# Fourteen transformer sublayers on one core: identity matmuls with unread results taken out of TensorE's orders

## The chip, the cores and the metric

The kernel runs on one core of one Trainium2 chip, in one launch. The metric is the device time of that core in microseconds (us), lower is better. The engines are named as in the profile: PE is TensorE, DVE is VectorE, ACT is ScalarE, POOL is GpSimd and SP is SyncE. Each has its own instruction queue and runs it in order; they meet over semaphores.

## The reference

The input x is 4 sequences of 512 tokens of width 128. The reference runs twelve sublayers with residuals over it, x + sublayer(layernorm(x)), in a sandwich pattern: a half-weighted feed-forward, an attention, the same feed-forward again, at four levels.

```
x = x + 0.5 * L0_ffn(LN(x)); x = x + L0_attn(LN(x)); x = x + 0.5 * L0_ffn(LN(x))
x = x + 0.5 * L1_ffn(LN(x)); x = x + L1_attn(LN(x)); x = x + 0.5 * L1_ffn(LN(x))
x = x + 0.5 * L2_ffn(LN(x)); x = x + L2_attn(LN(x)); x = x + 0.5 * L2_ffn(LN(x))
x = x + 0.5 * L3_ffn(LN(x)); x = x + L3_attn(LN(x)); x = x + 0.5 * L3_ffn(LN(x))
```

- L0_ffn scores 1024 patterns, takes the top eighth, then the top of 512 processing units, a softmax, and the top of 1024 output patterns. "Top" is found by ranking. L0_attn is causal with relative positions, 16 heads of width 8.
- L1_ffn is itself a causal attention and a mixture of 8 experts with the top 2. L1_attn is a linear causal attention: normalized q and k, a gate beta, no softmax.
- L2_ffn is a mixture of 8 experts with the top 1; L2_attn is causal inside blocks of 32 tokens, with rotation.
- L3_ffn is two transformer layers (8 heads of 64, windows of 64, a gated feed-forward); L3_attn is full attention with rotation.

## The kernel before

**Units and slots.** The twelve sublayers become 14 (each L3_ffn is two layers), and each is done per sequence, except that L2_ffn takes two at a time: 52 units in all. Every unit has three parts. The *pre* part normalizes and makes the heads, the *core* part does the attention or the ranking, the *post* part projects and adds to x. Slot k runs the core of unit k, the pre part of unit k+1 and the post part of unit k-1 side by side. Slots run from -1 to 52. Slots -1 to 2 are blocks of their own, each ended by a barrier; from slot 3 on one block holds all.

**Streams and orders.** In a slot each of those parts is a stream of generator functions, one for each engine. A stream is a letter: a is the core (where there is one), b the pre part, c the post part, and further letters are small extras. A generator's step ends at a `yield`. `in_order` (line 202) runs the steps of an engine in an order written out by hand in the table ORDERS (line 2558): "a5b1" means five steps of stream a, then one of b. SLOT_ORDERS maps the slot to its entry. An engine can't overtake in this order: if the next step waits, all behind it waits.

**The fillers.** The last letter of TensorE's order in twelve of the slots is a stream of its own, made by `fillers` (line 257). Each of its steps is one matmul of the bf16 identity with two copies of the identity, 256 columns:

```
nc.tensor.matmul(out, m.identb, m.identb.unsqueeze(1).to_broadcast([P, FILL // P, P]), start=True, stop=True)
```

The result goes to the right half of a PSUM bank that is not in use in that slot (bank 2, 3, 4, 5 or 6), and is never read. It signals nothing. How many there are is counted from the order string:

```
n = sum(c for i, c in runs(order) if i == len(streams))
```

The first filler of a slot first waits for the end of the core part of the slot before, as the stream is given `before.core`. A filler costs a weight load and a matmul on TensorE and nothing on any other engine.

**Lines that come up.** L265 is the filler matmul. In the L0_ffn: L388 are the four transposes after the normalization (all sublayers use it), L886 the scores of the 1024 patterns (16 matmul instructions, 512 columns), L839 to L842 VectorE's comparisons for the ranking and L850 to L852 the matmuls that sum them, L945 and L1036 the matmuls of its core. In the attentions: L439 makes q, k and v, L586 turns the stacked heads (L550 and L598 copy them out of PSUM), L1456 and L1470 belong to the core of L0_attn, L1747, L1760 and L1765 to that of L1_attn. L663 is the projection of an attention's output. In the last unit's post part: L2502 is the first matmul of the gated feed-forward (six groups of 512 columns, each drained by ScalarE at L2518 or by VectorE at L2530 before the next may start), L2508 the second one (24 matmuls), L307 its bias row.

Of the kernel before, what the change touches and what calls it, by code (L numbers as in the profile page):

```python
# [2461 lines left out]
def l3_layer_post(nc, m, lane, a, b, l):  # L2462
# [82 lines left out]
    def done(eng):  # L2545
        eng.wait_ge(lane.taken, lane.n)
        if l == DEPTH - 1:
# [10 lines left out]
ORDERS = [  # L2558
    {"tensor": "b17a1b3a1b2a1b6a1b1a5b1a2b20a1b3a1b6a1b6a1b1a1b9a1b4a1b2a1",
     "vector": "a13",  # L2560
     "scalar": "a11",
     "gpsimd": "a1"},
# [12 lines left out]
     "scalar": "c2b2a1b7a1b2a1",  # L2575
     "gpsimd": "b1",
     "sync": "f9d1f13e1d1f2a1f8"},
    {"tensor": "a5b1a1b1a1b1a1b1d7b1d12c2d1b1d6c1b2a1d1c1d2a1d4b1c1d4a1d1a1b1d2a1d6b1a1c1a1d3b1d1c1d1a1d6b1a2b1d1b1c"
               "1b1a1b1c2a1c1a1d10",
     "vector": "b4a2b5a1c2a1b1a1c1a1b1a1c2a1b1c2b1c3b1",  # L2580
     "scalar": "b3a1b4c1b1c1b1a1b7a1",
     "gpsimd": "b6",
     "sync": "b1a1b4"},
    {"tensor": "a1b1a1d1b1d1c1d4b1d1b1d1a1d2b1c1d7b1a1c1d1a1b1d7a2b1d1a1d10b1d2c1d1c1d1b1d1a2d1c1a1d1b1d3a1d3b1a1d1a"
               "1c1b1d1a1d4b1a1c1b1d7b1d1c1d1a1d1b1c1d13c1a1d1a2d2a2d3a1d1a1",
     "vector": "b3a1b1a6b5c2a2b1a1c1a3b1c1a3b1c1a2b1c2a2c1a3b1c1a1c1",
     "scalar": "b7a1c1a1c1b2a2b1a2b1a3b1a2b4a9",
     "gpsimd": "b6",
     "sync": "a4b5"},
    {"tensor": "b1c1a1b1e2c1e1b1e5b1e3b1e1a1e2a1e2c1e24b1e9b1e9b1e7a1e3b1e2a3b1a1c1e3b1e2a2b1e2a1e3b1e1c1e3a1e1b1a2b"  # L2590
               "1a1b1c1b1a3e1a2e5a3e5a1",
     "vector": "b4c1b1a1c1b3a1c1b1a4b1a3b1a4b1a1c1a3b1a7c1b1",
     "scalar": "b9a2b1a2b1a2b1a2c1a1b1a2b2a1b1a8",
     "gpsimd": "b6d1",
     "sync": "a4b5"},
    {"tensor": "b1c1b1a2e1b1a1e1b1e2c1b1e35c1a1e4a1e10c1b1e14b1e3b1e3a1e3a1b1a1e1c1e1b1e2c1b1e4a2b1e1a1e5a1b1e1a1e1a"
               "1e1b1e8b1a1e1b1e2a2e1b1e3a1e1a1e7a1e2a3e1a1",
     "vector": "b4c1a5c1a1b4c1b1a2c1a2b1a1b1a4b1a3b1c1a4b1a2",
     "scalar": "b4a1b5a3b1c1b1a4b1a2b1a1b2a2b1a7",
     "gpsimd": "b4d1b2",  # L2600
     "sync": "a4b5"},
    {"tensor": "e5c1b1e2a1b1e1c1e2a1e8b1e7b1c1e2b2e3b1e1a1b1e4a1e4a1e2c1e7b1a2e2a1e3b1e5b1e1a1e2a1e4c1a2e2b1e1b1e4b1"
               "e3a1e9b1e1a1e1b1a3b1e27b1e2a1c1a1e1b1e7a3e1a1e2a1",
     "vector": "b4a1c1a3c2a8c1a3b2a1b1a2b2a1b1a2b1a2b1a1c1b1",
     "scalar": "b7a4b2a1b1a1b1a3c1a11",
     "gpsimd": "d1b1",
# [3 lines left out]
     "scalar": "b11a2c1a1",  # L2610
     "gpsimd": "b1d1",
     "sync": "a1"},
    {"tensor": "e3c1a1c1a3b1c1a2c1a2b1e1c1b2e1b1c1b2a1b2a1e2c1a1e4c1e1b1a1b1c1e1a1e1b1a4b1a1c1e1b1e3b1a1b1a2b1c1b2",
     "vector": "b4c4a3c2a3c2a1b1a1b5c1b3c1",
     "scalar": "c2b2a1b7a1b2a1",
     "gpsimd": "b1d1",
# [30 lines left out]
               "c1b2a2c1a2b1c1a3c1b1a2c1a1c1b1c1b1c7",  # L2647
     "scalar": "b6a4c1a7c1a3b1c1b1a6b1a1b1a5b1a5b1a1b1a7b1a7",
     "gpsimd": "b2a1b1a1c1b1a1b2a1d1b1c1"},
    {"tensor": "e2c1e3a1e2c1e1b1a1e2c1b1e1a1c1a1c1b1e1c1a1b1e1a1e3b1e1a2c2e3a1e10c1e2a1e3a1e25c1e1a1e2c1b1e1a1c1a1b1"  # L2650
               "e1c1b1e2a1b1c1e4b1e3c1b1e1a1c1b1e5a1e1b1e9b1a1e29",
     "vector": "b3c1b1c1a2c1a1c1a1c4a2c2a1c1b3a1b4c1b4a1b3c1b1c1b1c1a1c2b1c1a1c1b1c1a1b1c1a1c1b1a1c1a1b1c2a1b1c4b1a1"
               "c4",
     "scalar": "b2c1b2a1b2c2b3a1b1a1b3a1b1",
     "gpsimd": "b1a1c1b5c1b1d1"},
    {"tensor": "e6a1c1b1e1a1e3b1e4a2b1c1b1e2b1a2c1e1a1e25a1e1a1e2c1e3a1e8a1e2a1e15b1e1a1b1a1b1e1a1e1b1e5b1a1b1e5b1a1"
               "b1e5b1a1e8",
     "vector": "b4a6b8a1b5a1b1a1b2a1b1a1b2a1c1a1b1a2b2a1b1a1",
     "scalar": "b6a1b1a1b3a1b4a1",
     "gpsimd": "b1d1a1b6"},  # L2660
    {"tensor": "e2a1c1a1b1e4b1a1b1a1b1a1b1a2e5a1c1e2a1c1e11a1e4c1e1a1e17a1e1b1e1a1b2e1a1b1e1a1e1b1e1a1e1b1e4b1a1b1a1"
               "b1e6",
     "vector": "b4a7b5a1b8a1b1a1b2a1b3c1a2b1a1b1a1b1a2b1",
     "scalar": "b6a2b5a1b2a1b1",
     "gpsimd": "b1d1a1b6"},
    {"tensor": "e1a2e2c1a1e2c1a1e8a1b1c1e6b1a1b1a1e1b1a1b1e4b1a1e8a1e3a1e12a1c1e2b1a1e6b1a1b1a1e3b1a1e3b1e1a2b1e1b1e"
               "14b1e2",
     "vector": "b2a2b1a2b2a1b5a3b1a1b1a1b2a2b1a1b1a2b1a1c1a1b2",
     "scalar": "b2a1b5a1b3a1b3a1",
     "gpsimd": "a1b7d1"},  # L2670
# [155 lines left out]
     "scalar": "a5b1a1b1a1b1a1b2a2",  # L2826
     "gpsimd": "c1b1",
     "sync": "b2"},
    {"tensor": "a4b64a1b3a2b7a1b4a1b8a1b6a1b7a1",
     "vector": "a12",  # L2830
     "scalar": "a5",
     "gpsimd": "a1",
# [611 lines left out]
```

## Time and profile before

| | us |
|---|---|
| median of 3 runs | 2942.89 (2940.99 to 2950.08) |
| profiled execution | 2941.67 |
| its span, first to last instruction | 2939.9 |
| TensorE matmuls busy | 2544.9 (87%) |
| VectorE busy | 2167.9 (74%) |
| ScalarE busy | 1664.1 (57%) |
| GpSimd busy | 787.8 (27%) |
| mean granted TensorE clock | 0.947 of full |

The page counts every matmul as busy, the unread ones too. The page's chain of work that ended last gives PE 45%, DVE 27%, ACT 10%, POOL 5% of the span. "Granted clock" is the share of its full clock that TensorE was given in a stretch: each moment it is 1.0 (2.4 GHz) or 0.5 (1.2 GHz), and a mean lies between. The views of stretches below give, for any stretch of the execution, each engine's busy time and this clock.

### The profile page before, as it was taken

The page shows a single profiled execution, that of the slowest core. Times are in us where ns is not written, and L with a number is a line of the kernel's source. Part 1 is how long each engine was busy: PE and PEld are TensorE (multiplying, and loading weights), DVE is VectorE, ACT ScalarE, POOL GpSimd, SP SyncE. Part 2 cuts the span into 40 slices and gives each one's busy share as a digit, 9 for nine tenths or more (in the row PEclk, how much of TensorE's full clock was granted, in tenths as well). Part 3 has the DMA queues.
Part 4 walks back from the last instruction along what each step waited for, and adds up shares of the span by engine and source line. Part 5 has one row for each costly group of instructions (what it writes and reads, how often), then busy time and mean ns, then how long its engine had stood idle before and what let it go on. Part 6 is the DMA issues. An engine that isn't in the chain of part 4 may idle for free.

```text
span 2939.9 us, 63499 instructions
## 1 busy us (share of the span) xinstructions
PE 2544.9 (87%) x24589; PEld 1617.3 (55%) x24589; DVE 2167.9 (74%) x5133; ACT 1664.1 (57%) x4036; POOL 787.8 (27%) x810
## 2 busy tenths in 40 slices
PE   6878889788898888988877988999988889989998
PEld 3556666554455544547755875565653222556655
DVE  4856557778887668877567567888877777888883
ACT  2334443466642367753476546767747666676773
POOL 1010001111111111121332246546511114455650
PEclk9879998899999999999999999999989998999999
DMA  3623420000000000014600661010100000001001
GB/s 114 243 41 57 81 62 1 1 1 1 1 1 1 1 1 1 1 58 168 252 6 1 216 217 30 15 28 17 28 3 3 1 1 13 16 16 28 18 19 28
DMA packets 123078, 131.95 MB, mean 45 GB/s; under 512 B 81941, under 2 KB 101653, under 8 KB 121242
## 3 DMA queue, kind: packets, MB, share of 16 engines
q1 hardware_dynamic: 120250, 122.70, 14.0%
q8 instruction: 196, 3.21, 0.5%
q0 software_dynamic: 2048, 4.20, 0.4%
q10 hardware_dynamic: 480, 0.98, 0.1%
q14 instruction: 104, 0.85, 0.1%
HBM read 80.73 MB, written 29.04 MB: 37 GB/s over the span
## 4 chain that ended last, share of the span: by engine, by line
PE 45%; DVE 27%; ACT 10%; issue 7%; POOL 5%; DMA 2%; SPq 0%; DVEq 0%; POOLq 0%; ACTq 0%
DVE nm L1251 6%; PE ps L1210 4%; PE ps L586 3%; PE ps L1990 3%; PE ps L1187 3%; PE ps L2199 3%; PE ps L1151 3%; PE ps L2365 2%; ACT hand L550 2%; PE ps L663 2%; PE ps L439 2%; DVE pre L2285 2%; PE ps L2502 2%; POOL ss L2276 1%; PE ps L265 1%
## 5 line engine op out<-in xcount | busy, mean ns | idle before, releaser
L1251 DVE TENSOR_REDUCE nm<-ps 128x2 f32<-128x256 f32 (+2 forms) x704 | 424.0, 636 | 65.3 <-PE ps L1151 42.4
L1300 ACT ACTIVATE core<-ps 128x512 f32<-128x512 f32 x672 | 358.7, 591 | 93.0 <-PE ps L1192 48.4
L380 POOL TENSOR_TENSOR rstd<-ve,weights 128x4 f32<-128x4 f32 x80 | 83.0, 1038 | 879.5 <-DVE ve L357 828.1
L2271 POOL TENSOR_TENSOR pre<-pre,sin 128x512 f32<-128x512 f32 x128 | 231.2, 1825 | 226.9 <-ACT pre L2242 200.1
L1151 PE MATMUL ps<-hand 128*128 128x128 bf16 (+4 forms) x1024 | 246.0, 314 | 44.9 <-DVE nm L1251 39.8
L550 ACT COPY hand<-ps 64x512 bf16<-64x512 bf16 x336 | 194.7, 579 | 132.1 <-PE ps L586 81.7
L1187 PE MATMUL ps<-hand 128*128 128x128 bf16 (+4 forms) x1024 | 225.3, 307 | 21.7 <-ACT hand L550 15.1
L2405 ACT ACTIVATE core<-ps,nm 128x128 f32<-128x128 f32 x512 | 181.9, 379 | 67.0 <-DVE nm L2422 66.0
L2276 POOL TENSOR_TENSOR ss<-ss,weights 128x16 f32<-128x16 f32 x64 | 196.6, 3072 | 71.6 <-DVE ss L2291 69.9
L2199 PE MATMUL ps<-weights,pre 128*128 128x512 f32 x384 | 200.0, 624 | 11.2 <-ACT hand L2253 6.6
L1261 POOL CAST hand<-nm 128x16 bf16<-128x16 f32 x192 | 59.0, 308 | 492.6 <-DVE nm L1251 484.3
L1210 PE MATMUL ps<-core,hand 128*32 128x512 f32 (+3 forms) x2048 | 179.4, 445 | 8.3 <-ACT otok L1283 5.6
L265 PE MATMUL ps<-identb 128*128 128x256 bf16 x1052 | 165.6, 286 | 16.9 <-PEq L3046 14.3
L1187 PEld LDWEIGHTS ps<-hand 128*128 128x128 bf16 (+1 forms) x1024 | 81.6, 98 | 179.1 <-ACT core L1300 94.9
L1151 PEld LDWEIGHTS ps<-hand 128*128 128x128 bf16 (+1 forms) x1024 | 86.1, 98 | 162.9 <-DVE nm L1251 112.4
L2365 PE MATMUL ps<-hand 64*64 64x128 f32 (+1 forms) x2048 | 136.2, 273 | 0.0
L2365 PEld LDWEIGHTS ps<-hand 64*64 64x64 f32 x2048 | 104.7, 135 | 44.4 <-issue 44.4
L265 PEld LDWEIGHTS ps<-identb 128*128 128x128 bf16 x1052 | 100.3, 102 | 50.5 <-issue 35.1
L586 PE MATMUL ps<-identb,hand 128*128 128x128 bf16 x768 | 79.4, 229 | 55.4 <-DVE pre L502 17.4
L2502 PE MATMUL ps<-post,weights 128*128 128x512 f32 (+1 forms) x192 | 105.6, 632 | 22.3 <-DVE post L2530 13.8
L2422 DVE TENSOR_REDUCE nm<-ps 128x4 f32<-128x512 f32 x128 | 87.2, 682 | 44.3 <-PE ps L2365 43.9
L2285 DVE TENSOR_TENSOR pre<-pre,cos 128x1024 f32<-128x1024 f32 x64 | 108.0, 1688 | 13.9 <-ACT pre L2242 13.8
(352 smaller groups left out, 6313.6 us busy)
## 6 DMA issues: line engine op xcount, KB each, us to landing
hand<-in_experts SPq DMA_DIRECT2D x48, 836.0 KB, 4.7
shear<-post SPq DMA_DIRECT2D x64, 256.0 KB
core<-in_experts SPq DMA_DIRECT2D x12, 836.0 KB, 5.1
core<-shear SPq DMA_DIRECT2D x128, 64.0 KB, 2.2
hand<-hand SPq DMA_DIRECT2D x16, 512.0 KB, 4.4
hand<-hand SPq DMA_DIRECT2D x16, 384.0 KB, 5.6
core<-in_stream SPq DMA_DIRECT2D x2, 2048.0 KB, 7.7
shear<-pre SPq DMA_DIRECT2D x16, 256.0 KB
```

The costliest lines, as they stand in the source:

```text
L265: nc.tensor.matmul(out, m.identb, m.identb.unsqueeze(1).to_broadcast([P, FILL // P, P]), start=True, stop=True)
L550: ins = copy(a.QX[64 * e:64 * e + 64, q_slot(2 * pair + e), :], src[64 * e:64 * e + 64, :])
L1151: ins = nc.tensor.matmul(b[:, n * nk:(n + 1) * nk], q[:, qt * P:(qt + 1) * P], k[:, lo:lo + nk], start=kind != BLOCK32 and n == 0, stop=Tr ...
L1187: ins = nc.tensor.matmul(b[:, n * w:(n + 1) * w], k[:, kt * P:(kt + 1) * P], q[:, s:z], start=kind != BLOCK32 and n == 0, stop=True, skip_ ...
L1210: ins = nc.tensor.matmul(m.ps[32 * j:32 * j + 32, OUT, s:z], a.V[:, kt, 9 * h:9 * h + 32], prob8[:, i % PROBS, n * w:(n + 1) * w], start=( ...
L1251: nc.vector.tensor_reduce(nm_of(unit), src, AX.X, ALU.max, negate=True).then_inc(negmax, 1)
L1300: nc.scalar.activation(prob8[:, i % PROBS, 0:w], m.ps[:, RING[at % NR], 0:w], ACT.Exp).then_inc(ring_out, 1)
L2199: nc.tensor.matmul(banks[at % N], s.hT[:, t * P:(t + 1) * P], qkv[:, l, i, :], start=True, stop=True).then_inc(lane.filled, 1)
L2271: ins = nc.gpsimd.tensor_tensor(o[:, :, :, z:z + hl], x[:, :, :, y0:y0 + hl], sn[:, t, :, z:z + hl].unsqueeze(2).to_broadcast([P, 2, LH, h ...
L2276: nc.gpsimd.tensor_tensor(m.ss[:, 1, 0:2 * LH], m.ss[:, 0, 0:2 * LH], m.weight["half"][:, 0:2 * LH], ALU.pow).then_inc(rooted, 1)
L2365: ins = nc.tensor.matmul(out[rows, r * P + at:(r + 1) * P], a.Q3[rows, c, n * WIN:(n + 1) * WIN], a.K3[rows, c, lo:(n + 1) * WIN], start=F ...
L2405: nc.scalar.activation(prob[:, i % NP3, r * P:(r + 1) * P], bank(m, S[i % 2])[:, r * P:(r + 1) * P], ACT.Exp, bias=m.nm[:, 4 * i + r:4 * i ...
```

## The change

In twelve entries of ORDERS the steps of the filler stream are taken out of TensorE's string; the remaining steps keep their order. As the number of fillers is counted from the string, the stream is then empty and no such matmul is made. The slots and their numbers of fillers: -1 (81), 3 (68), 4 (85), 5 (96), 6 (119), 7 (126), 9 (18), 16 (119), 17 (99), 18 (63), 19 (79), 52 (99), 1052 in all. Slots 4 to 7 hold the cores of L0_attn, 16 to 19 those of L1_attn; slot -1 is the first pre part alone and slot 52 the last post part alone. The orders of the other engines are not touched. The diff, with three of the twelve entries (the other nine are of the same kind):

```
-    {"tensor": "b17a1b3a1b2a1b6a1b1a5b1a2b20a1b3a1b6a1b6a1b1a1b9a1b4a1b2a1",
+    {"tensor": "a19",
...
-    {"tensor": "a5b1a1b1a1b1a1b1d7b1d12c2d1b1d6c1b2a1d1c1d2a1d4b1c1d4a1d1a1b1d2a1d6b1a1c1a1d3b1d1c1d1a1d6b1a2b1d1b1c"
-               "1b1a1b1c2a1c1a1d10",
+    {"tensor": "a5b1a1b1a1b1a1b2c2b1c1b2a1c1a1b1c1a2b1a1b1a1c1a1b1c1a1b1a2b2c1b1a1b1c2a1c1a1",
...
-    {"tensor": "a4b64a1b3a2b7a1b4a1b8a1b6a1b7a1",
+    {"tensor": "a12",
```

## Rows read from the trace of the kernel before

**Rows 1.** the page: the span line, and the fillers' row of part 5
```profile
span 2939.9 us, 63499 instructions
...
L265 PE MATMUL ps<-identb 128*128 128x256 bf16 x1052 | 165.6, 286 | 16.9 <-PEq L3046 14.3
```

**Rows 2.** stretches, L265 alone: us, busy (count), clock, DMA share, GB/s
```profile
155.00:203.00 48.00, 12.16 (x68) 0.79 0.21 38
...
203.00:410.00 207.00, 70.05 (x426) 0.93 0.34 61
...
835.00:1045.00 210.00, 54.64 (x360) 0.98 0.01 1
...
2911.00:2940.00 29.00, 11.95 (x99) 1.00 0.06 14
```

**Rows 3.** stretches, all engines: us, busy (count) of each, clock, DMA
```profile
155.00:203.00 48.00, 34.90 (x390) 27.14 (x389) 27.78 (x82) 18.09 (x38) 5.42 (x7) 0.79 0.21 38
...
203.00:410.00 207.00, 173.21 (x4313) 131.28 (x4313) 131.25 (x297) 101.41 (x205) 15.20 (x15) 0.93 0.34 61
...
835.00:1045.00 210.00, 184.58 (x1853) 118.74 (x1849) 154.32 (x365) 61.76 (x126) 38.35 (x45) 0.98 0.01 1
...
500.00:560.00 60.00, 43.87 (x369) 33.44 (x367) 44.44 (x125) 17.67 (x38) 13.61 (x11) 0.72 0.00 1
```

**Rows 4.** chain by line, stretches 145:410, 810:1045 and 2905:2940
```profile
by line: PE ps L265 12.4%; PE ps L586 7.6%; PE ps L1470 6.9%; issue 6.5%; ACT hand L550 4.6%; DMA shear<-pre 4.5%; PE ps L439 4.4%; PE ps L1456 4.1%; PE ps L945 3.6%; PE ps L1350 3.0%; ACT hand L598 2.7%; PE ps L886 2.5%; PE ps L1447 2.4%; 
by line: issue 12.6%; PE ps L586 6.4%; PE ps L1586 5.3%; DVE core L1791 4.5%; PE ps L1648 3.8%; PE ps L1765 3.7%; DVE y L1603 3.7%; PE ps L1760 3.3%; PE ps L265 3.2%; PE ps L1210 3.0%; DVE pre L362 2.5%; PE ps L1747 2.5%; DVE y L362 2.4%; D
by line: PE ps L2502 19.2%; PE ps L663 10.9%; PE ps L2508 8.4%; DMA out<-x 6.5%; DMA post<-y 4.9%; PE ps L265 4.7%; DVE post L2530 4.3%; DVE x L2540 4.0%; ACT post L2518 4.0%; issue 3.4%; PE ps L388 2.9%; POOL rstd L380 2.9%; SPq L2473 2.6%
```

**Rows 5.** timeline at three filler runs: start, us, engine, line
```profile
276.51 2.13 PE L265 MATMUL ps<-identb 128*128 128x256 bf16 x9
...
277.62 0.42 DVE L598 COPY hand<-ps 128x512 bf16<-128x512 bf16 x1
...
398.44 3.11 PE L265 MATMUL ps<-identb 128*128 128x256 bf16 x27
...
400.05 0.35 DVE L842 SCALAR_TENSOR_TENSOR pre<-pre,acc_pre,weights 128x128 bf16<-128x128 f32 x1
...
862.83 2.31 PE L265 MATMUL ps<-identb 128*128 128x256 bf16 x10
```

**Rows 6.** short stretches, L265 alone, columns as in Rows 2
```profile
319.00:322.40 3.40, 3.40 (x33) 1.00 0.70 130
...
2913.10:2916.50 3.40, 3.40 (x33) 1.00 0.19 39
```

**Rows 7.** short stretches at the low clock, all engines
```profile
42.40:52.70 10.30, 4.36 (x5) 1.83 (x6) 1.12 (x4) 0.00 (x0) 0.71 (x1) 0.50 0.99 409
...
858.40:865.00 6.60, 6.30 (x37) 4.46 (x38) 6.26 (x19) 1.76 (x3) 0.00 (x0) 0.50 0.01 2
...
527.20:554.40 27.20, 18.64 (x157) 17.14 (x158) 14.06 (x35) 9.49 (x17) 2.15 (x3) 0.50 0.00 1
```

**Rows 8.** chain by line, stretch 527:555
```profile
by line: PE ps L586 28.3%; PE ps L1036 12.6%; ACT hand L550 8.3%; PE ps L965 8.2%; DVE hand L550 7.5%; DVE pre L498 6.1%; ACT hand L598 4.2%; DVE pre L490 3.7%; PE ps L954 3.4%; DVE hand L598 3.1%; PE ps L956 3.0%; DVE hand L501 2.6%; PE ps
```

**Rows 9.** timeline of TensorE at the start
```profile
14.29 3.78 PE L265 MATMUL ps<-identb 128*128 128x256 bf16 x17 [14.29 <-PEq L3046]
...
23.17 4.83 PE L886 MATMUL ps<-pre,weights 128*128 128x512 f32 x10
...
48.34 2.07 PE L945 MATMUL ps<-core,wv 128*128 128x512 f32 x2 [8.93 <-DMA core<-in_stream]
```

**Rows 10.** timeline of TensorE near the end, and one row at 472 us
```profile
2921.03 1.13 PE L2502 MATMUL ps<-post,weights 128*128 128x512 f32 x2 [0.62 <-ACT post L397]
...
2932.57 2.94 PE L2508 MATMUL ps<-weights,post 128*128 128x128 f32 x24
...
472.07 3.76 PE L1036 MATMUL ps<-post,wv_post 128*128 128x128 f32 x16
```

More of the change, by code:

```diff
@@ L2583 @@
      "sync": "b1a1b4"},
-    {"tensor": "a1b1a1d1b1d1c1d4b1d1b1d1a1d2b1c1d7b1a1c1d1a1b1d7a2b1d1a1d10b1d2c1d1c1d1b1d1a2d1c1a1d1b1d3a1d3b1a1d1a"
-               "1c1b1d1a1d4b1a1c1b1d7b1d1c1d1a1d1b1c1d13c1a1d1a2d2a2d3a1d1a1",
+    {"tensor": "a1b1a1b1c1b2a1b1c1b1a1c1a1b1a2b1a1b1c2b1a2c1a1b1a1b1a2c1b1a1b1a1c1b2c1a1b1c2a7",
      "vector": "b3a1b1a6b5c2a2b1a1c1a3b1c1a3b1c1a2b1c2a2c1a3b1c1a1c1",
@@ L2589 @@
      "sync": "a4b5"},
-    {"tensor": "b1c1a1b1e2c1e1b1e5b1e3b1e1a1e2a1e2c1e24b1e9b1e9b1e7a1e3b1e2a3b1a1c1e3b1e2a2b1e2a1e3b1e1c1e3a1e1b1a2b"
-               "1a1b1c1b1a3e1a2e5a3e5a1",
+    {"tensor": "b1c1a1b1c1b3a2c1b3a1b1a3b1a1c1b1a2b1a1b1c1a1b1a2b1a1b1c1b1a9",
      "vector": "b4c1b1a1c1b3a1c1b1a4b1a3b1a4b1a1c1a3b1a7c1b1",
@@ L2595 @@
      "sync": "a4b5"},
-    {"tensor": "b1c1b1a2e1b1a1e1b1e2c1b1e35c1a1e4a1e10c1b1e14b1e3b1e3a1e3a1b1a1e1c1e1b1e2c1b1e4a2b1e1a1e5a1b1e1a1e1a"
-               "1e1b1e8b1a1e1b1e2a2e1b1e3a1e1a1e7a1e2a3e1a1",
+    {"tensor": "b1c1b1a2b1a1b1c1b1c1a2c1b3a2b1a1c1b1c1b1a2b1a2b1a2b2a1b1a2b1a7",
      "vector": "b4c1a5c1a1b4c1b1a2c1a2b1a1b1a4b1a3b1c1a4b1a2",
@@ L2601 @@
      "sync": "a4b5"},
-    {"tensor": "e5c1b1e2a1b1e1c1e2a1e8b1e7b1c1e2b2e3b1e1a1b1e4a1e4a1e2c1e7b1a2e2a1e3b1e5b1e1a1e2a1e4c1a2e2b1e1b1e4b1"
-               "e3a1e9b1e1a1e1b1a3b1e27b1e2a1c1a1e1b1e7a3e1a1e2a1",
+    {"tensor": "c1b1a1b1c1a1b2c1b3a1b1a2c1b1a3b2a2c1a2b3a1b1a1b1a3b2a1c1a1b1a5",
      "vector": "b4a1c1a3c2a8c1a3b2a1b1a2b2a1b1a2b1a2b1a1c1b1",
@@ L2612 @@
      "sync": "a1"},
-    {"tensor": "e3c1a1c1a3b1c1a2c1a2b1e1c1b2e1b1c1b2a1b2a1e2c1a1e4c1e1b1a1b1c1e1a1e1b1a4b1a1c1e1b1e3b1a1b1a2b1c1b2",
+    {"tensor": "c1a1c1a3b1c1a2c1a2b1c1b3c1b2a1b2a1c1a1c1b1a1b1c1a1b1a4b1a1c1b2a1b1a2b1c1b2",
      "vector": "b4c4a3c2a3c2a1b1a1b5c1b3c1",
@@ L2649 @@
      "gpsimd": "b2a1b1a1c1b1a1b2a1d1b1c1"},
-    {"tensor": "e2c1e3a1e2c1e1b1a1e2c1b1e1a1c1a1c1b1e1c1a1b1e1a1e3b1e1a2c2e3a1e10c1e2a1e3a1e25c1e1a1e2c1b1e1a1c1a1b1"
-               "e1c1b1e2a1b1c1e4b1e3c1b1e1a1c1b1e5a1e1b1e9b1a1e29",
+    {"tensor": "c1a1c1b1a1c1b1a1c1a1c1b1c1a1b1a1b1a2c2a1c1a2c1a1c1b1a1c1a1b1c1b1a1b1c1b1c1b1a1c1b1a1b2a1",
      "vector": "b3c1b1c1a2c1a1c1a1c4a2c2a1c1b3a1b4c1b4a1b3c1b1c1b1c1a1c2b1c1a1c1b1c1a1b1c1a1c1b1a1c1a1b1c2a1b1c4b1a1"
@@ L2655 @@
      "gpsimd": "b1a1c1b5c1b1d1"},
-    {"tensor": "e6a1c1b1e1a1e3b1e4a2b1c1b1e2b1a2c1e1a1e25a1e1a1e2c1e3a1e8a1e2a1e15b1e1a1b1a1b1e1a1e1b1e5b1a1b1e5b1a1"
-               "b1e5b1a1e8",
+    {"tensor": "a1c1b1a1b1a2b1c1b2a2c1a3c1a3b1a1b1a1b1a1b2a1b2a1b2a1",
      "vector": "b4a6b8a1b5a1b1a1b2a1b1a1b2a1c1a1b1a2b2a1b1a1",
@@ L2660 @@
      "gpsimd": "b1d1a1b6"},
-    {"tensor": "e2a1c1a1b1e4b1a1b1a1b1a1b1a2e5a1c1e2a1c1e11a1e4c1e1a1e17a1e1b1e1a1b2e1a1b1e1a1e1b1e1a1e1b1e4b1a1b1a1"
-               "b1e6",
+    {"tensor": "a1c1a1b2a1b1a1b1a1b1a3c1a1c1a1c1a2b1a1b2a1b1a1b1a1b2a1b1a1b1",
      "vector": "b4a7b5a1b8a1b1a1b2a1b3c1a2b1a1b1a1b1a2b1",
@@ L2665 @@
      "gpsimd": "b1d1a1b6"},
-    {"tensor": "e1a2e2c1a1e2c1a1e8a1b1c1e6b1a1b1a1e1b1a1b1e4b1a1e8a1e3a1e12a1c1e2b1a1e6b1a1b1a1e3b1a1e3b1e1a2b1e1b1e"
-               "14b1e2",
+    {"tensor": "a2c1a1c1a2b1c1b1a1b1a1b1a1b2a4c1b1a1b1a1b1a1b1a1b1a2b3",
      "vector": "b2a2b1a2b2a1b5a3b1a1b1a1b2a2b1a1b1a2b1a1c1a1b2",
```

## The prediction

> **What bounds the kernel now.** I read the page first. The one group of instructions that goes away is TensorE's row of line 265: 1052 matmuls into a PSUM corner that nobody reads, 165.6 us busy [rows 1]. Their busy time is not their price. They fill places in which TensorE would otherwise wait, and what they are worth either way depends on two things: whether useful work stands behind them, and whether they hold TensorE's clock up. So I next asked for the stretches that hold fillers. Besides 81 at the start they lie in 155 to 203 us (68), 203 to 410 (426), 835 to 1045 (360) and 2911 to 2940 (99), and 18 around 440 to 470 [rows 2]. In 203 to 410 us TensorE is busy 173.2 us, 70.0 of it in fillers, so 103.2 of 207 us is useful work; in 835 to 1045 it is 129.9 of 210 [rows 2, 3]. The granted clock is 0.79, 0.93 and 0.98 there. Beside them I put a stretch with no filler, 500 to 560 us: TensorE is busy 43.9 of 60 us with useful work alone, and its clock is 0.72 [rows 3]. The two levels are 1.0 (2.4 GHz) and 0.5 (1.2 GHz), so a mean of 0.72 means that 56% of the stretch was spent at the low one.
>
> Then the chain of waits says what is on the path. Fillers hold 12.4% of the chain in 145 to 410 us (32.9 us), 3.2% in 810 to 1045 (7.5) and 4.7% in 2905 to 2940 (1.6) [rows 4]. Elsewhere the chain there is a mixture: no engine bounds these stages alone, TensorE hands over to ScalarE or VectorE after each group.
>
> **Term 1, the queue gets shorter (gain).** The chain gives 32.9 + 7.5 = 40.4 us to fillers in the middle slots. That is an upper bound: the chain walks back through all fillers of a run if the useful matmul behind them was ready by the time that the last one ended, even if it had become ready only just before. Three runs show the real delay [rows 5]. At 398.44 us 27 fillers end at 401.55; the rank matmul behind them needs VectorE's L842, done at 400.40, so 1.15 of 3.11 us was delay. At 276.51 nine fillers end at 278.64; the transposes behind need a copy that ends at 278.04: 0.60 of 2.13. At 862.83 ten fillers take 2.31 us and no producer ends inside: I count all of it. Sum 4.06 of 7.55, 54%; applied to 40.4 us this is about 20 to 22. VectorE and ScalarE work close behind (154 and 62 us of 210 in the third stretch [rows 3]), so when TensorE comes earlier they are late next; I take 16. Bounds: 0 and 40. I cost the removed weight loads and the one wait for the earlier core that the first filler of each slot carried at nothing: the matmuls of the same slots carry the same wait, and should this cover be gone the price is inside the 40.
>
> **Term 2, the clock in the middle slots (loss).** Fillers are put where useful work is thin. In 319.0 to 322.4 us they are all that TensorE does (33 of them) at clock 1.0 [rows 6]; I found nine more places in the three middle stretches where they make up half or more of TensorE's work. Where work was thin and nothing filled it, the clock was low: 527.2 to 554.4 at 0.50 with TensorE busy 18.6 of 27.2 us, after an idle spell; and even 858.4 to 865.0, where it was busy 6.3 of 6.6 [rows 7]. I expect eight of the ten places to drop. A spell lasts 6.6 us in the second of those rows and 27.2 in the third; I take 8 each, nearer the short one, as dense work follows: 64 us more at 1.2 GHz. What is one us of it worth? In 527 to 555 the chain gives TensorE at least 55.5% (28.3 + 12.6 + 8.2 + 3.4 + 3.0) [rows 8]; half of this would be saved at the high clock, 0.28 us per us. 64 x 0.28 = 18, and I take 17. Bounds: no spell added, 0; and 56% of the 465 us low, as in 500 to 560. That would be 260 us, of which 20.2 + 29.0 + 8.4 = 58 are low already (twice the missing clock times the length [rows 3]); 202 x 0.28 = 57.
>
> By the Trainium skill, page "TensorE: Matmul & The Clock Gate", section "Why this matters for your kernels", the drop in mid-kernel comes from idle gaps of TensorE between bursts of matmuls. By this rule alone the middle slots, which have few long idle gaps, would lose nothing, and the sum would be 17 us lower, which is rival A below. The trace agrees only in part: 858.4 to 865.0 us stood at 0.50 with TensorE busy 6.3 of 6.6 us [rows 7].
>
> **Term 3, the start (loss).** The first 17 fillers run at 14.29 us in 3.78 us, 0.22 us apiece against 3.11 / 27 = 0.12 later [rows 5, 9], so they run at the low level while the first normalization is under way, and useful work finds the high one. Without them the scores matmuls L886 are the first dense work. At the second start of TensorE, at 48.34 after a DMA, the low level held until 52.7: 4.4 us of work [rows 7, 9]. A pair takes 2.07 us there, while ten take 4.83 at the high level (0.97 a pair). So about 4.4 us of work run at half speed: +2.2 us. All of the first slot stands ahead of a barrier and of the DMA of the next weights, for which TensorE waits 8.93 us; nothing hides it. Bounds 1 and 4.
>
> **Term 4, the last slot (loss).** After the last projection ends at about 2911.4, 64 fillers bridge the shift of the tokens and the normalization; in 2913.1 to 2916.5 they are all there is [rows 6]. Without them I expect the low level from there to nearly the end. Behind stand six pairs of 512-column matmuls on the chain, each 1.13 us [rows 10] and 2.07 at the low level [rows 9]: 6 x 0.94 = 5.6. Then 24 matmuls L2508 in 2.94 us; 16 of the same shape took 3.76 at 472 us, a low place, so 24 would take 5.6: +2.7. Transposes and the bias row add 0.5. Sum +8.8, with no gain from the removed fillers, as ScalarE's and VectorE's drains of 0.7 us set when each pair can start. Bounds 3 (the clock comes back after the first pairs) and 10.
>
> **Sum** against the profiled execution (2941.67 us; span 2939.9): 2941.7 - 16 + 17 + 2.2 + 8.8 = 2953.7. The median of the runs shown is 2942.89, 1.2 above it; I predict 2954.
>
> **Rivals.** *A, the clock holds in the middle.* Useful work at 50% to 62% of the time keeps it up except where it falls today. For it: clock 0.98 in 835 to 1045, whose fillers are thin. Against: 500 to 560. Then 2941.7 + 11 - 20 = 2933, faster; with the whole 40 us, 2913.  Chance 0.19.
> *B, the low level becomes the rule in the attention slots.* In 203 to 410 us TensorE waits after every group for a copy, and a level once lost needs dense work to come back: 27.2 us at 0.50 [rows 7]. Then 2941.7 + 11 - 16 + 57 = 2994. It decides from about 150 us of added low time. Against: at the low clock the same work fills more of the time, and spells of 3 to 7 us are the common ones. Chance 0.13.
> *C, the two middle terms and the ends cancel.* Half of the spells (8 us) against a gain of 20: 2941.7 + 11 - 20 + 8 = 2941. Chance 0.25.
> That the change doesn't do what it says I exclude: the number of fillers is counted from the order string. Forecast: 0.43.
>
> **Numbers.** Predicted 2954. Range 2930 to 2986: it takes in A's likely part and C, and B's lower half. The forecast's own range is 2946 to 2966. What can be told from no change is 0.3%, 9 us. Faster than 2934: A's 0.19 and 0.01 of C, 0.2. Within: the other 0.24 of C and 0.07 for the forecast's edge below 2952, 0.31. Slower: 0.36 of the forecast and B, 0.49.
>
> **What would show it.** Term 1: useful groups behind former fillers start earlier, and VectorE is the releaser. Term 2: mean clock below 0.90 in the two long stretches, with new places at 0.5. Term 3: the pairs L886 at 19.5 us take about 2 us, and the first L945 starts near 50.5. Term 4: pairs L2502 near 2.07 us in the last 20 us. I am wrong if the mean clock stays near 0.947, or if 203 to 410 gets shorter by more than 15 us.

## The result

The changed kernel takes 2970.24 us (median of 5 runs, 2967.39 to 2973.78) against 2942.89 (2940.99 to 2950.08): ratio 1.0094, 95% interval 1.0079 to 1.0109, so it is slower by 23 to 32 us. The forecast was slower, 2954, with a range up to 2986. The sign and the ends of the sum were right; the middle was not: +1 was forecast for the two middle terms together and +21 came in slots 3 to 19.

The page of the changed kernel: span, TensorE's busy time, and the granted clock in 40 slices (tenths).

```profile
span 2967.6 us, 61325 instructions
...
PE 2477.9 (84%) x23468; PEld 1561.8 (53%) x23537; DVE 2167.7 (73%) x5133; ACT 1663.9 (56%) x4036; POOL 786.5 (27%) x810
...
PEclk8867788799988889998999989999999999999997
```

The clock's slices in the page of before:

```profile
PEclk9879998899999999999999999999989998999999
```

TensorE's busy time falls by 67 us, while the fillers' busy time was 165.6 [rows 1]: the useful matmuls were busy longer. A slice is some 74 us. The clock is lower in slices 3 to 6 (slots 3 to 7), in 12 to 15 (slots 16 to 19) and in the first and the last one, and nearly as before elsewhere.

All useful instructions are the same in both kernels and stand in the same order on TensorE. So every trace was cut at the same useful weight loads, those that start at 48.3, 156.4, 410.0, 835.9, 1045.1, 2904.2 and 2935.1 us in the profile of before. The table gives the change of each stage's length in us and, in brackets, the time at 1.2 GHz before and after. These lows are twice the missing clock times the length, or the sum of the low spells that the trace holds. The first row has none, as the trace's record of the clock begins only at 18.6 us (24.1 in the changed kernel).

| stage of before | what runs | change | low clock, us |
|---|---|---|---|
| 0 to 48.3 | slot -1 and the wait for the DMA | +1.1 | |
| 48.3 to 156.4 | slots 0 to 2 | +0.8 | (39, 40) |
| 156.4 to 410.0 | slots 3 to 7, 494 fillers | +1.3 | (51, 140) |
| 410.0 to 835.9 | slots 8 to 15, 18 fillers | +5.6 | (55, 75) |
| 835.9 to 1045.1 | slots 16 to 19, 360 fillers | +14.0 | (10, 82) |
| 1045.1 to 2904.2 | no filler in before | -4.8 | (154, 140) |
| 2904.2 to 2935.1 | end of slot 51, slot 52 | +9.5 | (0, 30) |

Stretches of the changed kernel, all engines, columns as in [rows 3]; they are the third, fifth and last stage:

```profile
158.40:413.30 254.90, 172.08 (x4205) 130.20 (x4204) 159.34 (x377) 118.46 (x240) 20.67 (x22) 0.73 0.32 57
...
844.70:1067.90 223.20, 166.18 (x1486) 100.37 (x1486) 153.83 (x363) 60.95 (x124) 38.51 (x45) 0.82 0.00 1
...
2922.20:2962.70 40.50, 24.95 (x103) 14.48 (x103) 7.58 (x22) 5.09 (x8) 1.01 (x1) 0.62 0.04 10
```

The same three stages of before, cut at the same instructions:

```profile
156.40:410.00 253.60, 206.71 (x4699) 157.92 (x4698) 159.04 (x377) 118.90 (x240) 20.62 (x22) 0.90 0.32 57
...
835.90:1045.10 209.20, 183.72 (x1849) 118.73 (x1847) 153.50 (x363) 60.85 (x124) 38.40 (x45) 0.98 0.01 1
...
2904.20:2935.10 30.90, 26.13 (x202) 18.96 (x202) 7.51 (x22) 5.09 (x8) 1.01 (x1) 1.00 0.05 14
```

Read the first line of each: the clock went from 0.90 to 0.73 and the stage got 1.3 us longer. In the second it went from 0.98 to 0.82 and the stage got 14.0 us longer. VectorE has the same busy time in both; it waits more.

The start, TensorE in order of time, answers to [rows 9]:

```profile
17.21 1.25 PE L388 MATMUL ps<-weights,pre 128*128 128x128 f32 x4 [17.21 <-DVE pre L362]
...
19.14 9.95 PE L886 MATMUL ps<-pre,weights 128*128 128x512 f32 x16 [0.68 <-ACT pre L395]
...
49.48 2.93 PE L945 MATMUL ps<-core,wv 128*128 128x512 f32 x3 [8.97 <-DMA core<-in_stream]
```

The sixteen scores matmuls take 9.95 us in one piece, where [rows 9] has ten in 4.83. With the fillers between them the sixteen went from 19.50 to 28.0. The first L945 starts 1.1 us later. The forecast's sign for this term is met in part: the first pairs ran at the low level (two matmuls every 1.7 us up to about 24 us, behind it every 0.9 to 1.0), but L945 starts at 49.48 and not near 50.5.

The end answers to [rows 10]:

```profile
2938.57 1.15 PE L388 MATMUL ps<-weights,post 128*128 128x128 f32 x4 [7.51 <-DVE post L362]
...
2940.68 2.08 PE L2502 MATMUL ps<-post,weights 128*128 128x512 f32 x2 [0.95 <-ACT post L397]
...
2957.84 5.37 PE L2508 MATMUL ps<-weights,post 128*128 128x128 f32 x24 [0.84 <-DVE post L2530]
```

The pair takes 2.08 us instead of 1.13, and the 24 matmuls 5.37 instead of 2.94. Ahead of them TensorE is idle for 7.51 us, where 64 fillers ran.

Who waited for whom on TensorE in slots 16 to 19 of the changed kernel (total us, times, longest):

```profile
PE ps L1765 <- DVE core L1791: 14.3, 12, 3.2
...
PE ps L388 <- DVE pre L362: 6.3, 3, 3.3
```

and in before:

```profile
PE ps L1765 <- DVE core L1791: 4.6, 7, 1.2
```

The wait behind VectorE's L1791 tripled. Time that fillers had covered now shows as idle time of TensorE, and what it does between the waits runs at the low clock for 82 of the 223 us.

### The profile page after: what moved, and what is told of

It reads as the page before. It is cut to its first block, busy times and chain, and to the rows that moved or that the text cites. A ratio compares the mean times of both kernels' runs of the same rounds, so it can differ in the third digit from the quotient of the medians.

```text
span 2967.6 us, 61325 instructions
## 1 busy us (share of the span) xinstructions
PE 2477.9 (84%) x23468; PEld 1561.8 (53%) x23537; DVE 2167.7 (73%) x5133; ACT 1663.9 (56%) x4036; POOL 786.5 (27%) x810
## 4 chain that ended last, share of the span: by engine, by line
PE 44%; DVE 27%; ACT 10%; issue 7%; POOL 4%; DMA 2%; SPq 0%; another core or an unknown queue 0%; DVEq 0%; ACTq 0%; POOLq 0%
DVE nm L1251 6%; PE ps L1210 3%; PE ps L586 3%; PE ps L2199 3%; PE ps L1990 3%; PE ps L1187 3%; PE ps L1151 3%; PE ps L2365 2%; ACT hand L550 2%; PE ps L663 2%; PE ps L439 2%; PE ps L2502 2%; DVE y L1603 2%; DVE pre L2285 2%; PE ps L945 1%
## 5 line engine op out<-in xcount | busy, mean ns | idle before, releaser
L1151 PE MATMUL ps<-hand 128*128 128x128 bf16 (+4 forms) x997 | 237.2, 313 | 44.1 <-DVE nm L1251 38.9
L1187 PE MATMUL ps<-hand 128*128 128x128 bf16 (+4 forms) x1005 | 219.1, 307 | 18.5 <-ACT hand L550 11.2
L586 PEld LDWEIGHTS ps<-identb,hand 128*128 128x128 bf16 x768 | 51.5, 105 | 128.1 <-ACT hand L598 37.1
L1603 DVE SCALAR_TENSOR_TENSOR y<-ps,sel_post,y 128x128 f32<-128x128 f32 x256 | 89.3, 350 | 40.0 <-PE ps L299 16.7
```

The lines of the kernel that those rows point to most:

```text
L586: ins = nc.tensor.transpose(lane.atb[:, side * L + t * P:side * L + (t + 1) * P], pair_of(stk, t, pair), m.identb)
L1151: ins = nc.tensor.matmul(b[:, n * nk:(n + 1) * nk], q[:, qt * P:(qt + 1) * P], k[:, lo:lo + nk], start=kind != BLOCK32 and n == 0, stop=Tr ...
L1187: ins = nc.tensor.matmul(b[:, n * w:(n + 1) * w], k[:, kt * P:(kt + 1) * P], q[:, s:z], start=kind != BLOCK32 and n == 0, stop=True, skip_ ...
```

## The experiments

Every kernel below is the kernel before with the edit shown; `...` marks what is left out of an edit. Each is compared with executions of the kernel before from the same session, so that time differs a little (2941.00 to 2945.41 us). One function takes the fillers of one slot out of its order, or multiplies them: `with_fillers(order, letter, times)`. FILLED gives the letter of the filler stream in each slot. "Stages" are the differences of stage lengths in one profiled execution each, cut as above.

**1. One region at a time.**

```
+for k in (-1,):                   # e_start
+for k in (52,):                   # e_end
+for k in (3, 4, 5, 6, 7, 9):      # e_l0
+for k in (16, 17, 18, 19):        # e_l1
+    o = ORDERS[SLOT_ORDERS[k]]
+    o["tensor"] = with_fillers(o["tensor"], FILLED[k], lambda n: 0)
```

> Only the 81 fillers of slot -1 are taken out. Theory (each region pays for its own clock and nothing is shared): 1.5 to 2.5 us slower than before, as the first scores matmuls run at 1.2 GHz; everything behind slot 0 is as before. Rival (the start is hidden behind the DMA of the weights that TensorE waits for at 48 us): no change, under 0.5 us.

Measured: 2944.36 against 2941.59 us, ratio 1.0012 (1.0000 to 1.0024). In the profile the first L945 comes 1.5 us later. The time alone hardly tells it from no change, nor from the rival; the place of the delay does. In the five kernels of these experiments that change nothing ahead of slot 3 (`e_end`, `e_l0`, `e_l1`, `f_double`, `g_trim`) the first L945 comes between 0.6 us earlier and 0.3 us later. The theory holds, at the low end of its 1.5 to 2.5 us.

> Only the 99 fillers of slot 52 are taken out. Theory: 8.5 to 10 us slower, all of it behind the last projection: six pairs of 512-column matmuls at about 2.07 instead of 1.13 us and the 24 matmuls behind them at about 5.4 instead of 2.9. Rival (part of the 9.6 us that the last slot lost in the changed kernel came from its different start): under 6 us.

Measured: 2950.41 against 2941.59, ratio 1.0034 (1.0023 to 1.0045). The last stage is 8.1 us longer, low clock 27 us of it, and has the rows of the changed kernel:

```profile
2917.89 1.15 PE L388 MATMUL ps<-weights,post 128*128 128x128 f32 x4 [7.51 <-DVE post L362]
...
2919.99 2.08 PE L2502 MATMUL ps<-post,weights 128*128 128x512 f32 x2 [0.95 <-ACT post L397]
...
2937.15 5.49 PE L2508 MATMUL ps<-weights,post 128*128 128x128 f32 x24 [0.84 <-DVE post L2530]
```

The interval is 7 to 13 us, so the rival (under 6) is out. The theory holds, at the low end of what it allowed: the last slot's loss is its own.

> Only the fillers of slots 3 to 7 and 9 are taken out (512 of them). Theory (shorter queue against lower clock, almost in balance): 155 to 410 us takes 0 to 3 us longer although some 90 us more of it run at 1.2 GHz, and the L0_ffn slots behind up to 500 us some 3 us longer; total +2 to +6 us. Rival 1 (these slots are faster without fillers, and the changed kernel only hid it by chance): faster by 3 us or more. Rival 2 (the balance in the changed kernel was chance the other way): slower by 10 us or more.

Measured: 2952.63 against 2941.59, ratio 1.0034 (1.0020 to 1.0048), which is 6 to 14 us. In the profile 156 to 410 got 7.8 us longer and 410 to 836 5.8.

```profile
157.20:418.60 261.40, 177.44 (x4205) 133.97 (x4204) 159.26 (x377) 118.84 (x240) 20.74 (x22) 0.69 0.31 55
```

That is more than the theory's 0 to 3 us for the first part, and its total of 2 to 6 us is missed as well: the median is 11 us slower, where rival 2 begins. The runs do not decide for rival 2, as the interval begins at 6. The second part repeats the changed kernel's 5.6. Experiment 4 takes this up.

> Only the fillers of slots 16 to 19 are taken out (360 of them). Theory: 835 to 1045 us takes 11 to 16 us longer, with some 70 us more at 1.2 GHz; total +11 to +16 us. Rival (the place of the low spells is chance, and slots 1000 to 1045 just met a bad one in the changed kernel, 7 of the 14 us): +4 to +8 us.

Measured: 2957.36 against 2941.59, ratio 1.0055 (1.0038 to 1.0072), 11 to 21 us. The stage got 16.2 us longer (theory 11 to 16), with 79 us at the low clock:

```profile
837.10:1062.40 225.30, 166.71 (x1488) 100.08 (x1486) 153.77 (x363) 60.88 (x124) 38.51 (x45) 0.83 0.00 1
```

The rival's 4 to 8 us is out. The forecast had these slots, at clock 0.98, as the ones with least to lose; it was the fillers that held them there.

The four regions alone cost 2.8 + 8.8 + 11.0 + 15.8 = 38 us by their medians, all together 27. With the uncertainty of four ratios (some 8 us) and of the changed kernel's (4) this is only just more than chance, so the prices of the regions need not add up. With `h_start_l0` of experiment 4 in place of the first and the third it is 5.9 + 8.8 + 15.8 = 31 us, which agrees.

**2. Same places, fewer columns; and twice as many.**

```
-    out = m.ps[:, bank, L - FILL:L].rearrange("p (a b) -> p a b", b=P)
+    out = m.ps[:, bank, L - FILL:L - FILL + 16]
-            nc.tensor.matmul(out, m.identb, m.identb.unsqueeze(1).to_broadcast([P, FILL // P, P]), start=True, stop=True)
+            nc.tensor.matmul(out, m.identb, m.identb[:, 0:16], start=True, stop=True)
```

> All 1052 fillers stay where they are, but each streams 16 columns of the identity instead of 256. Its weight load of 128 columns (0.10 us) stays, so TensorE's queue is nearly as long as before, while little streams through the array. It parts the two terms: thin against before is the clock alone, thin against the changed kernel is the queue alone. Theory: the clock falls as in the changed kernel (mean 0.91 to 0.92) and the time is the worst of the three: 2970 plus what the queue costs, 8 to 20 us, so 2978 to 2990. Rival (it is the presence of any instruction that holds the clock): as before, 2943. Rival (the fillers' queue costs nothing): 2970, as the changed kernel.

Measured: 2981.56 against 2945.41, ratio 1.0135 (1.0113 to 1.0157); mean clock 0.913 in the profiled execution (the fastest of four, 2972.99 us) and 0.907 to 0.911 in the others, the changed kernel's is 0.912 (0.911 to 0.913). The two ratios differ by 0.0041, 12 us, with an uncertainty of about 8. The two long stages:

```profile
159.10:418.90 259.80, 185.76 (x4700) 150.71 (x4699) 158.55 (x377) 118.69 (x240) 20.70 (x22) 0.72 0.32 56
...
849.30:1076.10 226.80, 179.23 (x1845) 114.60 (x1847) 153.83 (x363) 60.89 (x124) 38.57 (x45) 0.80 0.00 1
```

So 1052 instructions that stream little do not hold the clock, and the time is at least that of no fillers: the rival that any instruction holds it is out, and what the change took away was the stream of columns. As a measure of the whole queue the run fails, because its premise was wrong: 64 such fillers take 1.75 us at the high clock, 0.03 us each, not 0.10 (the second row is all engines in that stretch, with the clock at 1.00):

```profile
2934.21 1.75 PE L265 MATMUL ps<-identb 128*128 128x16 bf16 x64
...
2934.20:2936.00 1.80, 1.76 (x66) 1.65 (x63) 1.02 (x3) 0.00 (x0) 0.00 (x0) 1.00 0.00 0
```

The row of their weight loads (ns, least, median, most):

```profile
L265 PEld LDWEIGHTS ps<-identb x1052: 95/98/205, 14.2 to 2960.3; 128*128 128x128 bf16 x176
```

Their queue is about a quarter of the real one (0.10 to 0.12 us each at the high clock [rows 5, 6], 0.22 at the low one [rows 9]) or less. By the times it costs 4 to 20 us, and this alone speaks against the rival that it costs nothing. The stages don't settle it: against the first profile of the changed kernel they are 4.9 and 3.6 us longer, against the second one (experiment 4) 6.9 longer and 2.3 shorter.

```
+for k in (3, 4, 5, 6, 7, 9, 16, 17, 18, 19):
+    o["tensor"] = with_fillers(o["tensor"], FILLED[k], lambda n: 2 * n)
```

> Twice as many fillers in slots 3 to 7, 9 and 16 to 19, at the same places; the start and the end are as before. Where the clock is at 1.0 already, only the queue gets longer. Theory: 155 to 410 us gains some of its 50 us at 1.2 GHz back (up to 10 us) but pays the queue a second time, and 835 to 1045 pays the queue nearly alone; total 15 to 40 us slower than before. Rival (the fillers stand in places in which TensorE would wait anyway, so that doubling costs nothing): within 5 us of before.

Measured: 2987.92 against 2945.41, ratio 1.0157 (1.0138 to 1.0177), the slowest of all, with the highest clock of the profiled executions (0.955; 0.950 to 0.952 in its others).

```profile
156.50:432.30 275.80, 245.30 (x5193) 199.44 (x5192) 158.88 (x377) 118.94 (x240) 20.68 (x22) 0.96 0.30 53
...
863.70:1090.70 227.00, 212.94 (x2203) 151.11 (x2206) 152.19 (x363) 60.83 (x124) 38.29 (x45) 1.00 0.01 1
```

Here the clock stands at 0.96 and 1.00 and the stages are 22.2 and 17.8 us longer, 40 us in all: a longer queue costs, even where it raises the clock. The stage between them, with 36 fillers in slot 9 in place of 18, is 5.5 us longer. The first dose stands in more of TensorE's idle time than the second, so I read 40 as more than its price; that is argued, not shown.

**3. Can both be had?** In one kernel more fillers went into slots that had none and were at the low clock, in gaps of the trace; in the other each run was shortened by what ran on after the useful matmul behind it had been released.

```
 # g_more: slots 0, 2, 8, 10, 11; slot 11 for one
-    "c1a4c1a2b1a1b1a1b1c1b2a1c1b1a1c1a1c1b1a1b1a1c1b1a2c1b1a1c1b1a4c1a1b2c1b1"
+    "c1a4c1a2b1a1e5b1a1b1c1e3b1e5b1a1c1b1a1c1a1e3c1e44b1a1e14b1a1c1b1a2c1e4b1a1c1e3b1a4c1a1b1e10b1c1b1"
...
 # g_trim has ten such orders; here, in place of the code, the number of fillers left out by slot:
 # 3: 24, 4: 13, 5: 27, 6: 55, 7: 51, 9: 6, 16: 56, 17: 38, 18: 31, 19: 37
```

> All fillers of before stay, and slots 0, 2, 8, 10 and 11 get 86, 18, 26, 12 and 91 more, placed where TensorE idled in the trace of before (0.125 us of gap for each). In before these slots spend 67 us at 1.2 GHz. Theory (a filler pays where it stands in idle time of a stretch that is at the low level): clock near 1.0 in 500 to 555 us, 3 to 10 us faster than before. Rival (the price of the low level is as small there as in the L0_attn slots, 0.07 us for each us, and the queue takes it back): within 3 us of before.

Measured: 2941.47 against 2941.00, ratio 1.0005 (0.9991 to 1.0020). Two stretches of it, and the first of them in before:

```profile
40.00:52.00 12.00, 9.26 (x64) 6.84 (x65) 2.62 (x13) 0.00 (x0) 1.01 (x1) 0.91 0.91 348
...
500.00:560.00 60.00, 55.90 (x515) 42.64 (x514) 46.17 (x131) 21.25 (x43) 12.32 (x11) 0.83 0.01 1
```

```profile
40.00:52.00 12.00, 3.66 (x5) 1.59 (x6) 2.62 (x13) 0.00 (x0) 1.01 (x1) 0.60 0.89 350
```

The clock rose from 0.60 to 0.91 around the second start and from 0.72 to 0.83 in 500 to 560 us, and nothing came of it in the total: 410 to 836 is 0.3 us shorter, and the first L945 comes 1.1 us later, not earlier. Inside, between the same weight loads, the part from 500 to 560 us of before is 1.9 us shorter and the part from there to 836 is 1.5 us longer; whether the second has to do with the first is open. The rival holds. VectorE is busy 46 of 60 us in that stretch.

> In slots 3 to 7, 9 and 16 to 19, 338 of the 872 fillers are taken out: in each run the last ones, as many as ran on after the semaphore of the useful matmul behind them had been signalled. Theory (the queue part can be had without the clock part): clock stays above 0.93, 3 to 9 us faster than before. Rival (these fillers hold the clock as well as the others do): mean clock 0.92 to 0.93 and 0 to 10 us slower.

Measured: 2953.04 against 2941.00, ratio 1.0049 (1.0032 to 1.0067).

```profile
842.30:1058.30 216.00, 175.07 (x1682) 109.91 (x1683) 153.43 (x363) 60.79 (x124) 38.51 (x45) 0.91 0.01 1
```

The rival holds here too: in slots 16 to 19 the clock fell from 0.98 to 0.91 and the stage got 6.8 us longer, although only the delaying fillers had gone. The 162 of 360 (45%) that went cost 42% of what taking all of them cost there (16.2 in `e_l1`; other profiles give 14.0 and 19.9, so 34% to 49%). Slots 3 to 7 got 2.3 us longer, with 38 us more at the low clock. So the fillers that delay were about as good at holding the clock as the others.

**4. How repeatable is a stage?** The changed kernel's profile had 203 to 410 us 0.4 us longer, `e_l0` 7.3.

```
+for k in (-1, 3, 4, 5, 6, 7, 9):  # h_start_l0; h_again is the changed kernel itself
```

> The fillers of slots -1, 3 to 7 and 9 are taken out; 16 to 19 and 52 keep theirs. In the profile of the changed kernel 203 to 410 us took 0.4 us longer, with slots 3 to 7 and 9 alone 7.3. Theory A (the later start moves the chip's decisions on the clock against the work, and this is repeatable): 203 to 410 takes 0 to 2 us longer, as in the changed kernel; total +9 to +13. Theory B (the same kernel meets the low spells at other places from execution to execution): anything from 0 to 8 us there, unlike the profile of the changed kernel in the placement of its spells.

Measured: 2946.99 against 2941.14, ratio 1.0023 (1.0010 to 1.0036), 3 to 11 us, mostly below the 9 to 13 that theory A gave for the total; but 203 to 410 took 0.3 us longer, with 94 us low (98 in the changed kernel), as theory A has it.

> The changed kernel once more, one look with a profile. Theory A: 203 to 410 us takes 0 to 1 us longer than in before and 835 to 1045 us 13 to 15, as in the first profile. Theory B: the stages differ from the first profile by several us either way, up to 7 in 203 to 410 and 4 in 835 to 1045, with the total within 2966 to 2975.

Measured: one run, 2972.83 us.

```profile
158.40:411.30 252.90, 171.40 (x4205) 129.72 (x4204) 158.53 (x377) 118.83 (x240) 20.78 (x22) 0.72 0.31 57
...
841.90:1071.00 229.10, 169.34 (x1485) 101.92 (x1487) 153.92 (x363) 60.93 (x124) 38.52 (x45) 0.81 0.00 1
```

Here 203 to 410 got 1.3 us shorter than in before, and 835.9 to 1045.1 19.9 us longer, against 14.0 in the first profile. The lows are 140 and 89 us. So the first stage repeats within 2 us when the start is changed as well (three profiles: +0.4, +0.3, -1.3) and was 7.3 once when it was not; the second spreads over 14.0, 16.2 and 19.9. The 13 to 15 us of theory A for the second stage are missed by 5, and the 5.9 us between the two profiles is more than the 4 of theory B. One profile is too few to hold a stage's price to better than some 3 us. Whether the start's shift of 1 us is what moves the spells in slots 4 to 7, or chance alone, one profile of `e_l0` can't say; nor do the times part `e_l0` (6 to 14 us) from `h_start_l0` (3 to 11). This stays open.

## Why the prediction was right, and where it was not

The sign, the range and the mechanism (a lower clock costs more than the shorter queue gains) came true. So did the sign named for term 2, a clock below 0.90 in the two long stretches (0.73 and 0.82). The size did not: 27 us against 12, and 2970 lies outside the 2946 to 2966 that the forecast gave as its own. It is inside the stated range because that reached to rival B, and partly by luck, as two errors in term 2 work against each other: far more low time than forecast, at a lower price.

- **Term 3, the start** (+2.2; bounds 1 and 4): right in kind, low in size: +1.1 and +1.2 in two profiles of the changed kernel, +1.5 in `e_start`, +0.9 in `h_start_l0`. Part of the low period was given back because the matmuls no longer stand behind fillers: the sixteen start 0.36 us earlier and have no others between them.
- **Term 4, the end** (+8.8): right. +9.5 in the changed kernel and +8.1 where it stood alone, pairs at 2.08 us against a forecast of 2.07, and the 24 matmuls 2.4 us longer against 2.7.
- **Term 2, the clock in the middle** (+17, from 64 us more at 1.2 GHz at 0.28 us each): the mechanism is shown, the size is not right. Where I forecast 64 us more low time there were 89 + 72 = 161, not far from the bound of 202, and another 20 in the stage between. The step that failed is the count of spells: I counted ten places at which fillers stand nearly alone and let eight of them drop for 8 us. The trace has nine low spells in slots 3 to 7 alone (140 us, the longest 47.8) and ten in slots 16 to 19 (82 us). The low level also came between the places that I had counted, where useful work was there but thin, and stayed longer than 8 us; that it stayed because no filler helped to bring the clock back is my reading, not shown. The stretch at clock 0.72, 56% of it low [rows 3], was the better guide: slots 3 to 7 came to 55%, slots 16 to 19 to 37%.
- **Its price**: if the shorter queue gave the 16 us forecast, the 181 us cost 1.3 + 5.6 + 14.0 = 20.9, + 16 = 37 us, 0.20 each, not 0.28. This is an estimate, as no run shows the 16. The 0.28 came from one stretch in which TensorE holds at least 55.5% of the chain [rows 8]. Slots 3 to 7 have 89 us more for +1.3, slots 16 to 19 have 72 for +14.0. Slots 3 to 7 also held the larger queue on the chain (32.9 of 40.4 us [rows 4]), and DMA and ScalarE are on their chain; how the difference divides between these two was not tried.
- **Term 1, the queue** (-16; bounds 0 and 40): neither confirmed nor refuted in size. A quarter of the queue costs 4 to 20 us (`f_thin`), a second dose costs 40 (`f_double`). Its sign is shown, and VectorE is the releaser, as forecast (L1791 in slots 16 to 19, 14.3 us against 4.6). Of the three runs of fillers from which I took 54%, two stood at the low clock (2.13 us for 9 and 2.31 for 10, against 3.11 for 27 [rows 5]), so they count the clock's price as the queue's.
- **Slots 8 to 15**: not in the forecast, +5.6. The 18 fillers of slot 9 lie there; both profiles in which slots 3 to 7 and 9 alone, or with the start, lost their fillers have it (+5.8, +5.5), and `e_l1` does not (+0.1). The second profile of the changed kernel has +4.7. It comes with the fillers of slots 3 to 9; but twice as many of them give +5.5 too (`f_double`), and slot 9 was not tried alone, so the cause is open.
- **The rest** (1045 to 2904): the same instructions took 4.8 us less. No kernel here has a filler in this stage, and its length differs from before by anything from -11.5 to +2.8 us among them (`e_start` and `g_more`). The place of low spells in it moves from profile to profile; I take the 4.8 for that.
- **Rival A** is out: the clock does not hold in the middle. **Rival B** was half right. The added low time, 161 us, is past the 150 that it named as its sign, so by that sign it is B, to which I gave 0.13, that came; but each us at the low clock cost less than B had it (0.20 by the estimate above, not 0.28), and 2994 was not reached. **Rival C** is out.
- By the Trainium skill, page "TensorE: Matmul & The Clock Gate", section "Why this matters for your kernels", the drop in mid-kernel comes from idle gaps between bursts of matmuls. The end agrees (7.51 us idle, then 2.08 us a pair). The middle agrees only in part: in slots 16 to 19 TensorE's longest wait was 3.3 us, and some of the low spells lie beside waits of 2.0 to 3.3 us. But in the last part of the stage, where no wait was longer than 1.9 us, the clock was low for some 31 of 48 us:

```profile
1013.90:1062.00 48.10, 37.16 (x306) 24.81 (x306) 24.90 (x53) 14.46 (x33) 6.27 (x4) 0.68 0.01 1
```

No version beat the kernel before; `g_more` equals it.

## What to carry to other kernels

Price dummy matmuls by place, not by their busy time. Here they paid at the end, where TensorE's own pairs are the chain (8 to 9.5 us for 99 of them), and where the chain has matmuls between short waits (14 to 20 us for 360); they paid little at the start (1 to 1.5 us for 81) and in slots 3 to 7, where other engines are on the chain as well (between -1 and 8 us for 494). To forecast what their removal does to the clock, look at a stretch of the same kernel that has equally thin work and none of them, and take its share of low time as the upper bound, rather than count the gaps. What a microsecond of low clock costs has to be asked of each stage by itself.

## What the runs showed of the hardware

- A raised clock can be worth nothing that the time shows: from 0.60 to 0.91 in 40 to 52 us, most of it a wait for a DMA, and from 0.72 to 0.83 in 500 to 560 us of `g_more`, for a ratio of 1.0005 (0.9991 to 1.0020).
- A matmul of 16 columns on a full weight load did not hold the clock: mean clock 0.913 with 1052 of them, 0.912 with none, 0.947 with 256 columns each (profiled executions of `f_thin`, the changed kernel and the kernel before).
- Sixty-four such small ones behind each other start 0.03 us apart at the high clock, though each weight load is shown with 0.10 us. The duration of one row is not its price in a queue.
